# Routing spread over several positions, and output rows added by PE and ACT in place of GpSimd

## The chip, the core and the metric

The kernel runs on one core of one Trainium2 chip. TensorE (PE), VectorE (DVE), ScalarE (ACT), GpSimd (POOL) and SyncE (SP, which only issues DMAs) each run their own list of instructions in order and meet through semaphores. The metric is device time in microseconds; less is better.

## The reference

The input x has 32 sequences of 256 positions and 256 features. What is computed, cut to what matters:

```python
x = x + attn(cond(x, cond_1024))         # causal attention over the 256 positions
y = cond2(x, cond_1024)                  # x + x @ layer, one 256x256 layer per sequence
h1 = y + proj(attention(layernorm(y)))   # over the 32 sequences: 16 heads, 4 of keys
probs = softmax(layernorm(h1) @ router)  # 8 experts, the best 2 are kept
out = x + h1 + moe(layernorm(h1))        # each kept row goes through its experts
```

Here `proj`, `layernorm` and `attention` carry the reference's weights, and `moe` gives each expert at most 2560 rows, in order of the rows.

## The kernel before

It has three stages.

The **opening** (`opening`) runs over the 32 sequences, two at a time (tiles u = 0 and 1), as a software pipeline of steps. A step k makes, for the pair k - 1, the rows x1 on DVE (L1038) from the attention product, the sum `whole` of the base layer and the pair's own (L1044, L1054), and the product of x1 with it, the rows x2. ACT copies x2 from PSUM beside x1 into the tile `x12` (L908), which has columns 0:D for x1 and D: for x2 and eight routing columns. SP stores the two parts into the tensor `x_rows` in DRAM with one DMA each (L568, L580), the x1 part early in the step and the x2 part at its end. At the end of a step DVE takes mean and variance of x2, POOL makes the reciprocal root (L940, L944), and DVE makes `shift` (L1116). Each engine's list has the steps one after the other, so `shift` of a step stands directly before x1 of the next. PE's score product of the new pair (L770 and the three lines of `three` after it) needs the low part of qT (L1027), which DVE makes after the small sums of L1054.

The **rows stage** (the first part of `rows_and_experts`) runs over 64 groups of 128 rows, two at a time, so in 32 positions. SP loads the rows of x_rows into the tile xg (`load`, L1301). At position k PE makes the scores of k (L1469), the projection of k - 2 into the bank `ps_h` (L1484), and turns the weights of k - 1 and multiplies them with the values (L1492, L1505). DVE takes the maxima (L1884), subtracts (L1889), adds projection and xg into `h1` (L1906) and makes the normalizing numbers. ACT makes the exponentials (L1688) and most copies, among them the turned weights (L1703), and writes normalized rows into `kept`. POOL multiplies the weights by their reciprocal sum (L1404), makes the roots, and adds the output rows `res = xg[:, 0:D] + h1` (L1399). SP may store `res` and load the next xg into the same tile only after that addition:

```python
                for u in places:
                    store(j, u)
                    load(j + 1, u)
```

**Routing** works on batches of four positions. When the logits of a batch are there, `choose(m)` on DVE (17 operations on 128x64 or less) finds the two best experts of each row and counts them. PE makes ranks from the counts (L1513), ACT copies them (L1670), and `place(m)` on DVE makes slots and weights (L1831 to L1862). DVE's `step` asks the two generators for one operation after each of its own instructions and runs what is left at the end of the position. From two positions after the choice on, POOL scatters the normalized rows of the batch to their slots, four indirect DMAs per position (L1418).

The **expert stage** runs 39 blocks of rows through two layers in three-part products on PE (L179 to L181), and POOL adds the results to the output in DRAM (L1440).

## Time and profile before

| | |
|---|---|
| three runs | 1207.85, 1207.9 and 1210.3 us, median 1207.9 |
| the profiled execution | 1198.41 us, of which the instructions span 1196.6 us |
| busy in the span | PE 91%, DVE 77%, ACT 66%, POOL 49% |
| mean granted clock of PE | 0.957 |

Busy shares are means over all three stages. A stage's own table of stretches tells which engine is full there. Matmuls are pipelined, so their busy time includes overlaps.

### The profile page before, as it was taken

Reading aid. Unit: us, or ns where it says so; the run is one execution under the profiler, and the core shown is the slowest. Engines: PE = TensorE matmul, PEld = TensorE weight load, DVE = VectorE, ACT = ScalarE, POOL = GpSimd, SP = SyncE. Lnnn points to the kernel's source line nnn. Section 1 sums busy time; section 2 is a strip of 40 time slices with the busy share of each in tenths; the row PEclk is TensorE's granted clock in tenths of the full one; section 3 lists DMA queues with packets and bytes.
Section 4 is the critical chain, followed back from the end, with each engine's and each line's share of the span. In section 5 each row is a group of like instructions: output and inputs, shape, how many; then the busy total and the mean of one; then the engine's idle time right before and its main releaser. Section 6 shows DMA issues by size and latency. Waiting matters only on the chain. (4 is left out here: it accounts for less than half of the span.)

```text
span 1196.6 us, 24516 instructions
## 1 busy us (share of the span) xinstructions
PE 1083.2 (91%) x7906; PEld 993.9 (83%) x7908; DVE 921.7 (77%) x2282; ACT 789.4 (66%) x1776; POOL 585.8 (49%) x568
## 2 busy tenths in 40 slices
PE   7899999999999887788877787899999999999994
PEld 4799999999998677677766765789998889889884
DVE  6677777777775689888998988897777777777772
ACT  2467767677775687677766766566667766776671
POOL 0022212122122154888887786488855554555446
PEclk9999999999999999889788988899999999999997
DMA  8433434334331023444444466478877677777654
GB/s 296 114 115 120 141 111 148 117 128 148 93 96 64 28 81 86 136 130 136 135 136 122 120 179 206 121 208 207 198 185 189 180 185 175 176 182 190 157 141 63
DMA packets 119017, 171.78 MB, mean 144 GB/s; under 512 B 14509, under 2 KB 90189, under 8 KB 118861
## 3 DMA queue, kind: packets, MB, share of 16 engines
q1 hardware_dynamic: 92300, 136.00, 37.1%
q0 software_dynamic: 26592, 34.24, 14.9%
q8 instruction: 64, 1.05, 0.4%
q14 instruction: 61, 0.49, 0.1%
HBM read 104.04 MB, written 67.97 MB: 144 GB/s over the span
## 5 line engine op out<-in xcount | busy, mean ns | idle before, releaser
L1440 POOL DMA_INDIRECT out_rows<-y,row x142 | 233.6, 1645 | 176.5 <-DVE y L2031 136.7
L1962 DVE TENSOR_TENSOR hl<-h,hh 128x512 fp32r<-128x512 f32 (+1 forms) x156 | 99.6, 642 | 84.7 <-ACT h L1641 84.2
L179 PE MATMUL gh<-w2h,hh 128*128 128x256 f32 x568 | 161.0, 284 | 1.1 <-issue 1.1
L181 PE MATMUL gh<-w2h,hl 128*128 128x256 f32 x568 | 161.1, 284 | 0.0
L180 PE MATMUL gh<-w2l,hh 128*128 128x256 f32 x568 | 161.0, 283 | 0.0
L1640 ACT ACTIVATE hh<-gw 128x512 fp32r<-128x512 f32 (+1 forms) x78 | 44.0, 564 | 128.4 <-issue 126.7
L1505 PE MATMUL gw<-pwT,vb 128*128 128x128 f32 x512 | 81.8, 326 | 50.8 <-ACT pwT L1703 48.5
L1418 POOL DMA_INDIRECT slot_rows<-kept,slot x104 | 109.2, 1050 | 29.1 <-issue 27.1
L1505 PEld LDWEIGHTS gw<-pwT,vb 128*128 128x128 f32 x512 | 74.8, 232 | 58.3 <-ACT pwT L1703 55.8
L179 PEld LDWEIGHTS gh<-w2h,hh 128*128 128x128 f32 x568 | 109.1, 192 | 2.3 <-issue 1.2
L180 PEld LDWEIGHTS gh<-w2l,hh 128*128 128x128 f32 x568 | 109.1, 192 | 1.2
L181 PEld LDWEIGHTS gh<-w2h,hl 128*128 128x128 f32 x568 | 109.1, 192 | 0.0
L936 POOL TENSOR_TENSOR layer_low<-whole,layer_high 128x528 fp32r<-128x528 f32 x32 | 41.6, 1320 | 127.2 <-ACT layer_high L856 127.2
L940 POOL TENSOR_SCALAR spread<-mv 128x2 f32<-128x2 f32 x32 | 6.9, 217 | 186.9 <-DVE mv L1110 185.5
L1469 PEld LDWEIGHTS gs<-kvd,qg 64*128 64x128 f32 x512 | 72.2, 202 | 4.4 <-ACT qg L1677 2.1
L1469 PE MATMUL gs<-kvd,qg 64*128 64x128 f32 x512 | 72.0, 284 | 1.2 <-DVE kvd L1874 0.7
L179 PE MATMUL gw<-xh,w1h 128*128 128x512 f32 (+1 forms) x156 | 64.2, 412 | 7.8 <-issue 6.8
L1404 POOL TENSOR_TENSOR pw<-pw,gden 128x512 f32<-128x512 f32 x64 | 65.6, 1042 | 9.5 <-DVE gden L1927 9.5
L1484 PE MATMUL gh<-wproj,aoT 128*128 128x264 f32 x256 | 67.4, 408 | 0.3 <-ACT ranks L1670 0.3
L1472 PE MATMUL gv<-cst,kvd 64*128 64x64 f32 x256 | 65.1, 282 | 0.0
L2031 DVE TENSOR_SCALAR y<-gh,weight 128x256 f32<-128x256 f32 x142 | 59.2, 477 | 5.9 <-PE gh L181 5.6
L1712 ACT COPY aoT<-gw 64x256 f32<-64x256 f32 x128 | 46.6, 364 | 24.7 <-PE gw L1505 22.9
(371 smaller groups left out, 3871.4 us busy)
## 6 DMA issues: line engine op xcount, KB each, us to landing
w1e<-in_moe_w SPq DMA_DIRECT2D x39, 512.0 KB, 5.9
w2e<-in_moe_w SPq DMA_DIRECT2D x39, 512.0 KB, 3.3
xr<-slot_rows SPq DMA_DIRECT2D x32, 532.0 KB, 5.7
xg<-x_rows SPq DMA_DIRECT2D x62, 260.0 KB, 3.4
x_rows<-x SPq DMA_DIRECT2D x32, 264.0 KB, 2.4
xT<-in_xT SPq DMA_DIRECT2D x32, 256.0 KB, 2.7
x<-in_x SPq DMA_DIRECT2D x32, 256.0 KB, 3.6
x_rows<-x SPq DMA_DIRECT2D x32, 256.0 KB, 2.5
```

What stands on the lines that cost most here:

```text
L179: nc.tensor.matmul(out, at_a(ah), at_b(bh), start=first, stop=False, skip_group_check=True)
L180: nc.tensor.matmul(out, at_a(ah), at_b(bl), start=False, stop=False, skip_group_check=True)
L181: return nc.tensor.matmul(out, at_a(al), at_b(bh), start=False, stop=last, skip_group_check=True)
L1404: g.tensor_tensor(pw[k % 2][u][:], pw[k % 2][u][:], den[:, u, :].unsqueeze(2) .broadcast_to([P, TG * NKV, S]), ALU.mult).then_inc(pool_did ...
L1418: g.indirect_dma_start(out=pr.slots, out_offset=bass.IndirectOffsetOnAxis(ap=pr.slot[:, c, j:j + 1], axis=0), in_=pr.rows[:, j, :], in_off ...
L1440: g.indirect_dma_start(out=out, out_offset=bass.IndirectOffsetOnAxis(ap=row[m % NR][:, t:t + 1], axis=0), in_=y[m % 2][:, t, :], in_offset ...
L1469: score = t_.matmul(ps_s[u][:, t * P:(t + 1) * P], qg[u][:, t].rearrange("p j s -> p (j s)"), kvd[u][0:KV1, t].rearrange("p g s -> p (g s) ...
L1472: turned_v = t_.transpose(ps_v[u][:, t * KV1:(t + 1) * KV1], kvd[u][KV1:P, t].rearrange("p g s -> p (g s)"), pr.cst[KV1:P, C_ID + KV1:C_ID ...
L1484: ins = t_.matmul(ps_h[u][:, 0:WIDE], aoT[u][:, h].rearrange("p t s -> p (t s)"), pr.wproj[:, h, :], start=(h == 0), stop=(h == 1))
L1505: ins = t_.matmul(ps_w[u][:, t * P:(t + 1) * P], vb[(k - 1) % 2][u][:, t, :], pwT[u][:, t].rearrange("p j s -> p (j s)"), start=True, stop ...
L1962: v.tensor_tensor(hl[m % 2][:, f, 0:n], h[:, f, 0:n], hh[m % 2][:, f, 0:n].bitcast(F32), ALU.subtract).then_inc(hl_did, 1)
L2031: v.tensor_scalar(y[m % 2][:, t, :], py[half][:, t % 2, :], weight[m % NR][:, t:t + 1], None, ALU.mult).then_inc(y_did, 1)
```

## The change

In the rows stage the output rows come from PE and ACT: the opening stores the sum x1 + x2 in the columns that held x1, PE adds these columns to the projection with a matmul by the identity after DVE has read the bank, and ACT copies the bank to `res`. POOL's addition goes. In the opening DVE makes the sum into the tile `whole` at the end of the step, and the store of it moves there; the next layer sum, which overwrites `whole`, waits for the store.

DVE's routing operations go through a queue that lasts over positions. `choose` joins it after the maxima, `place` at the start of a position, and nothing is run at the end of a position before the last ones. `place` handles both chosen experts in one operation where it took two. POOL's scatters come one position later.

```diff
                 if has(k - 1):
                     for u in places:
-                        after(sp, dve_did["x1"], k - 1, u)
-                        sp.dma_start(dst[seq(k - 1, u)][:, :, 0:D], x12[u][:, :, 0:D]).then_inc(stored1[u], 16)
...
                 if has(k - 1):
                     for u in places:
+                        after(sp, dve_did["sum"], k - 1, u)
+                        sp.dma_start(dst[seq(k - 1, u)][:, :, 0:D], whole[u][:, :, 0:D]).then_inc(stored1[u], 16)
                         after(sp, act_did["x2"], k - 1, u)
                         sp.dma_start(dst[seq(k - 1, u)][:, :, D:], x12[u][:, :, D:]).then_inc(stored2[u], 16)
...
                         dve.wait_ge(x_in[u], 16 * k)
-                        if k > 1:
-                            dve.wait_ge(stored1[u], 16 * (k - 1))
+                        after(dve, dve_did["sum"], k - 2, u)
                         for r in range(TC):
...
                         after(dve, pe_did["layer"], k - 1, u)
                         after(dve, pool_did["layer"], k - 2, u)
+                        if k > 1:
+                            dve.wait_ge(stored1[u], 16 * (k - 1))
                         v.tensor_tensor(whole[u][:, :, 0:D], pc[u][:].rearrange("p (c n) -> p c n", c=DC),
...
                         v.scalar_tensor_tensor(shift[:, u, :], mv[:, u, :, 0], -1.0, rstd[:, u, :],
                                                ALU.mult, ALU.mult).then_inc(dve_did["shift"], 1)
+                        after(dve, act_did["x2"], k - 1, u)
+                        after(dve, pool_did["layer"], k - 1, u)
+                        v.tensor_tensor(whole[u][:, :, 0:D], x12[u][:, :, 0:D], x12[u][:, :, D:2 * D], ALU.add
+                                        ).then_inc(dve_did["sum"], 1)
...
-                    due = first + n + DEPTH + 2 + part
+                    due = first + n + DEPTH + 3 + part
                     if k == (due if due < I2 - 1 else due + 2):
...
-                after(sp, pool_did["res"], j, u)
+                after(sp, act_did["res"], j, u)
                 sp.sem_inc(pr.passed, 1)
...
-                    for u in places:
-                        after(pool, dve_did["h1"], k - 2, u)
-                        if k > 2:
-                            pool.wait_ge(stored[u], 16 * (k - 2))
-                        g.tensor_tensor(res[u][:], rows12(k - 2, u)[:, 0:D], h1[u][:, 0:D], ALU.add
-                                        ).then_inc(pool_did["res"], 1)
...
-                        after(pe, dve_did["h1"], k - 3, u)
+                        after(pe, act_did["res"], k - 3, u)
...
+                if has(k - 2):
+                    for u in places:
+                        after(pe, dve_did["h1"], k - 2, u)
+                        t_.matmul(ps_h[u][:, 0:D], pr.ident, rows12(k - 2, u)[:, 0:D], start=False, stop=True,
+                                  skip_group_check=True).then_inc(pe_did["res"], 1)
                 for m in chosen_at(k - 1):
...
                     pe.wait_ge(chosen_did, m + 1)
-                    after(pe, dve_did["h1"], min(k - 2, I2 - 1), 0)
+                    after(pe, act_did["res"], min(k - 2, I2 - 1), 0)
...
+                if has(k - 2):
+                    for u in places:
+                        after(act, pe_did["res"], k - 2, u)
+                        if k > 2:
+                            act.wait_ge(stored[u], 16 * (k - 2))
+                        a.copy(res[u][:], ps_h[u][:, 0:D]).then_inc(act_did["res"], 1)
                 for m in chosen_at(k - 1):
                     take_ranks(m)
...
-            placing = {}
+            pending = deque()
+
+            def advance():
+
+                while pending and next(pending[0], pending) is pending:
+                    pending.popleft()
...
-                for k in range(K):
-                    rt.step(v.tensor_tensor(eq[:, 0:B], hot[:, k, 0:B], S1[:, 0:B], ALU.mult))
-                    yield
-                    rt.wait()
-                    rt.step(v.tensor_reduce(slotf[:, k, 0:B], eq[:, 0:B], AX.X, ALU.add))
-                    yield
-                    rt.wait()
+                rt.step(v.tensor_tensor(both[:, :, 0:B], hot[:, :, 0:B], S1[:, 0:B].unsqueeze(1).broadcast_to([P, K, B, E]),
+                                        ALU.mult))
+                yield
+                rt.wait()
+                rt.step(v.tensor_reduce(slotf[:, :, 0:B], both[:, :, 0:B], AX.X, ALU.add))
+                yield
+                rt.wait()
...
-                route = chain(*(placing.pop(m) for m in chosen_at(k - 2) if m != LAST_BATCH), *(choose(m) for m in chosen_at(k)))
+                pending.extend(place(m) for m in chosen_at(k - 2) if m != LAST_BATCH)
                 if score:
...
-                        next(route, None)
+                        advance()
+                pending.extend(choose(m) for m in chosen_at(k))
...
-                for _ in route:
-                    pass
-                for m in chosen_at(k - 1):
-                    if m != LAST_BATCH:
-                        placing[m] = place(m)
-                        next(placing[m])
+                while k >= I2 and pending:
+                    advance()
```

The other hunks say the same at more places: three waits of POOL at the end move by one position, `taken` is made by an addition in place of a copy, and the weights of a batch are made in one operation.

## Rows read from the trace of the kernel before

**Rows 1.** Stretches; columns: length, busy PE, PEld, DVE, ACT, POOL, clock, DMA, GB/s.

```profile
74.00:373.00 299.00, 299.00 (x2555) 299.00 (x2554) 220.37 (x561) 210.56 (x505) 63.74 (x88) 1.00 0.38 119
447.60:707.40 259.80, 208.92 (x1466) 182.32 (x1466) 232.67 (x641) 180.06 (x467) 203.95 (x242) 0.88 0.43 128
508.70:516.80 8.10, 7.51 (x64) 6.67 (x63) 8.06 (x29) 6.52 (x17) 6.17 (x8) 1.00 0.47 144
527.60:540.30 12.70, 8.62 (x53) 7.53 (x53) 12.18 (x36) 8.66 (x23) 11.35 (x14) 0.73 0.46 138
```

**Rows 2.** Line L1884, maxima: min/median/max ns, first and last start, two windows.

```profile
L1884 DVE TENSOR_REDUCE gmax<-gs x5: 627/681/692, 405.9 to 421.5; 128x16 f32<-128x512 f32 x5
...
L1884 DVE TENSOR_REDUCE gmax<-gs x52: 658/678/692, 447.6 to 708.7; 128x16 f32<-128x512 f32 x52
```

**Rows 3.** Timeline of DVE, rows stage; columns: start, us, idle before in brackets.

```profile
524.36 0.43 DVE L1906 TENSOR_TENSOR h<-gh,xg 128x264 f32<-128x264 f32 x1 [3.24 <-DMA xg<-x_rows]
...
538.32 1.03 DVE L1814 COPY taken<-chosen 128x64 bf16<-128x64 bf16 x1
```

**Rows 4.** Timeline of POOL, one position of the rows stage.

```profile
526.94 1.40 POOL L1399 TENSOR_TENSOR res<-xg,h 128x256 f32<-128x256 f32 x2
...
530.52 1.08 POOL L1418 DMA_INDIRECT slot_rows<-kept,slot  x1 [0.18 <-issue]
...
535.68 0.26 POOL L1391 TENSOR_SCALAR spread<-mv 128x2 f32<-128x2 f32 x1
...
536.78 1.40 POOL L1399 TENSOR_TENSOR res<-xg,h 128x256 f32<-128x256 f32 x2
```

**Rows 5.** Landings: first of L1301 (loads of xg), then of L568 (stores of x1).

```profile
DMA to landing us min/median/max: 2.7/3.4/5.3
...
DMA to landing us min/median/max: 2.2/2.5/4.5
```

**Rows 6.** Timeline of PE in position 2.

```profile
414.70 2.05 PE L1484 MATMUL gh<-wproj,aoT 128*128 128x264 f32 x8
416.59 1.04 PE L1492 MATMUL gw<-cst,pw 128*128 128x128 f32 x8
418.21 2.05 PE L1505 MATMUL gw<-pwT,vb 128*128 128x128 f32 x16 [0.58 <-ACT pwT L1703]
```

**Rows 7.** Timeline of ACT in position 2.

```profile
415.16 0.63 ACT L1688 ACTIVATE pw<-pw 128x512 f32<-128x512 f32 x1 [1.92 <-DVE pw L1889]
...
417.59 1.05 ACT L1703 COPY pwT<-gw 128x512 f32<-128x512 f32 x2
```

**Rows 8.** Timeline of DVE, start of position 3.

```profile
421.51 0.69 DVE L1884 TENSOR_REDUCE gmax<-gs 128x16 f32<-128x512 f32 x1 [0.36 <-PE gs L1469]
```

**Rows 9.** Timeline of POOL after the last position.

```profile
720.99 0.79 POOL L1391 TENSOR_SCALAR spread<-mv 128x2 f32<-128x2 f32 x1 [4.04 <-DVE mv L1916]
...
728.36 2.47 POOL L1399 TENSOR_TENSOR res<-kvd,h 128x256 f32<-128x256 f32 x2
731.00 1.09 POOL L1418 DMA_INDIRECT slot_rows<-kept,slot  x1 [0.17 <-issue]
```

**Rows 10.** Timeline of DVE, first block of experts.

```profile
740.60 2.49 DVE L1962 TENSOR_TENSOR hl<-h,hh 128x512 fp32r<-128x512 f32 x4
```

**Rows 11.** Timeline of DVE in the opening, from one step to the next.

```profile
266.94 0.16 DVE L1116 SCALAR_TENSOR_TENSOR shift<-mv,rstd 128x2 f32<-128x2 f32 x1 [0.94 <-POOL rstd L944]
267.13 1.66 DVE L1038 SCALAR_TENSOR_TENSOR x<-pa,rden,x 128x256 f32<-128x256 f32 x4
268.70 1.28 DVE L1044 TENSOR_TENSOR whole<-pc,base 128x512 f32<-128x512 f32 x2
270.34 0.40 DVE L1054 TENSOR_TENSOR whole<-pa,base 128x16 f32<-128x16 f32 x2 [0.36 <-PE pa L750]
270.66 1.28 DVE L1027 TENSOR_TENSOR qT_low<-pb,qT_high 128x512 fp32r<-128x512 f32 x2
```

**Rows 12.** Timeline of PE in the opening, first score of the new pair.

```profile
272.11 0.36 PE L770 MATMUL pa<-trir,identr 128*128 128x256 f32 x1
```

More of the change, by code:

```diff
@@ L1 @@
+from collections import deque
 from contextlib import ExitStack
-from itertools import chain
 import numpy as np
@@ L464, in opening @@
         pe_did = {n: sem(f"pe_{n}_") for n in "layer extra qT nT x1T score v kv q pT x2 y".split()}
-        dve_did = {n: sem(f"dve_{n}_") for n in "x1 layer extra qT nT x1T max rden u kv st mv shift v pT".split()}
+        dve_did = {n: sem(f"dve_{n}_") for n in "x1 layer extra qT nT x1T max rden u kv st mv shift sum v pT".split()}
         act_did = {n: sem(f"act_{n}_") for n in "layer qT nT x1T exp v uh q pT x2 nrm".split()}
@@ L564, in step @@
                         sp.dma_start(stack[u][0:STACK], pr.stacks[seq(k, u)]).then_inc(stack_in[u], 16)
-                if has(k - 1):
-                    for u in places:
-                        after(sp, dve_did["x1"], k - 1, u)
-                        sp.dma_start(dst[seq(k - 1, u)][:, :, 0:D], x12[u][:, :, 0:D]).then_inc(stored1[u], 16)
                 if has(k):
@@ L1206, in rows_and_experts @@
         x_in, stored, x_last = sems("g_x_in"), sems("g_stored"), sems("g_x_last")
-        pe_did = {n: sem(f"gpe_{n}_") for n in "score vT wT av h".split()}
+        pe_did = {n: sem(f"gpe_{n}_") for n in "score vT wT av h res".split()}
         dve_did = {n: sem(f"gdve_{n}_") for n in "max sub sum rden h1 st mv shift kv".split()}
-        act_did = {n: sem(f"gact_{n}_") for n in "q exp wT v ao logit nrm".split()}
-        pool_did = {n: sem(f"gpool_{n}_") for n in "soft res spread rstd".split()}
+        act_did = {n: sem(f"gact_{n}_") for n in "q exp wT v ao res logit nrm".split()}
+        pool_did = {n: sem(f"gpool_{n}_") for n in "soft spread rstd".split()}
         L2, eq, S1 = (sb(n, [P, BATCH, E]) for n in ("L2", "eq", "S1"))
@@ L1324, in step @@
                 for u in places:
-                    after(sp, pool_did["res"], j, u)
+                    after(sp, act_did["res"], j, u)
                     if j + 1 < LAST:
@@ L1481, in step @@
                         after(pe, act_did["ao"], k - 2, u)
-                        after(pe, dve_did["h1"], k - 3, u)
+                        after(pe, act_did["res"], k - 3, u)
                         for h in range(2):
                             ins = t_.matmul(ps_h[u][:, 0:WIDE], aoT[u][:, h].rearrange("p t s -> p (t s)"),
-                                            pr.wproj[:, h, :], start=(h == 0), stop=(h == 1))
+                                            pr.wproj[:, h, :], start=(h == 0), stop=(h == 1), skip_group_check=True)
                         ins.then_inc(pe_did["h"], 1)
@@ L1807, in choose @@
                 yield
+                rt.step(v.tensor_tensor(taken[:, :, 1:B + 1].rearrange("p e b -> p b e"), hot[:, 0, 0:B], hot[:, 1, 0:B],
+                                        ALU.add))
+                yield
                 if m == 0:
@@ L1811, in choose @@
                     rt.step(v.tensor_copy(taken[:, :, 0], before[:, :, 2 * BATCHES[m - 1][1]]))
-                yield
-                rt.wait()
-                rt.step(v.tensor_copy(taken[:, :, 1:B + 1].rearrange("p e b -> p b e"), pr.chosen[:, groups, :]))
                 yield
@@ L1855, in place @@
                 rt.wait()
-                for k, out in ((0, eq), (1, L2)):
-                    rt.step(v.tensor_tensor(out[:, 0:B], hot[:, k, 0:B], grow(prob[:, k, 0:B]), ALU.mult))
-                    yield
+                rt.step(v.tensor_tensor(both[:, :, 0:B], hot[:, :, 0:B], prob[:, :, 0:B].unsqueeze(3).broadcast_to([P, K, B, E]),
+                                        ALU.mult))
+                yield
                 rt.wait()
-                v.tensor_copy(pr.rows[:, groups, D:D + 2].bitcast(I32), pr.tok[:, groups, :])
+                rt.step(v.tensor_copy(pr.rows[:, groups, D:D + 2].bitcast(I32), pr.tok[:, groups, :]))
                 yield
-                v.tensor_tensor(pr.rows[:, groups, D + 2:ROW], eq[:, 0:B], L2[:, 0:B], ALU.add).then_inc(routed, 1)
+                rt.wait()
+                v.tensor_tensor(pr.rows[:, groups, D + 2:ROW], both[:, 0, 0:B], both[:, 1, 0:B], ALU.add).then_inc(routed, 1)
                 yield
@@ L1891, in step @@
                                         ALU.subtract).then_inc(dve_did["sub"], 1)
-                        next(route, None)
+                        advance()
+                pending.extend(choose(m) for m in chosen_at(k))
                 if has(k + 1):
@@ L1895, in step @@
                         heads(k + 1, u)
-                        next(route, None)
+                        advance()
                 if norm:
                     for u in places:
-                        after(dve, pool_did["res"], k - 3, u)
                         after(dve, act_did["nrm"], k - 3, u)
@@ L1907, in step @@
                                         ).then_inc(dve_did["h1"], 1)
-                        next(route, None)
+                        advance()
                     for u in places:
@@ L1911, in step @@
                         v.bn_stats(stats[:, u, :], h1[u][:, 0:D]).then_inc(dve_did["st"], 1)
-                        next(route, None)
+                        advance()
                     after(dve, pool_did["spread"], k - 3, U2 - 1)
@@ L1924, in step @@
                         v.tensor_reduce(den[:, u, :], pw[k % 2][u][:], AX.X, ALU.add).then_inc(dve_did["sum"], 1)
-                        next(route, None)
+                        advance()
                         after(dve, dve_did["sum"], k, u)
                         v.reciprocal(den[:, u, :], den[:, u, :]).then_inc(dve_did["rden"], 1)
-                        next(route, None)
+                        advance()
                 if norm:
```

12 lines of the change are left out of this document (6 added, 6 removed).

## The prediction

> **What bounds the kernel now.** I read the table of stretches first, because the shares of the whole span are a mean over three stages. In the opening the PE is busy for all 299.00 of 299.00 us at a granted clock of 1.00 [rows 1]: there a microsecond is lost for good if it is put between two matmuls, and nothing taken from another engine is won. In the middle stage, which makes the rows, no engine is full: in 447.6 to 707.4 PE has 208.92 of 259.80 us, DVE 232.67, POOL 203.95, and the clock is 0.88 [rows 1]. The first score maximum of each position marks its start. Positions 1 and 2, which route and scatter nothing, take (421.5 - 405.9) / 2 = 7.8 us; from position 6 to the start of position 31, where the last maximum but one stands 1.3 us before the 708.7 of the row, 25 positions take 259.8 us, 10.39 each [rows 2]. The expert stage after it is untouched in its order.
>
> Three things fill the gap between 7.8 and 10.39, one after the other in a cycle of four positions. First, where a batch is chosen (527.6 to 540.3) the position takes 12.7 us, DVE is busy for 12.18 of them, PE for 8.62, and the clock falls to 0.73 [rows 1]: all 17 routing operations go into this one position, the last of them behind DVE's other work, with PE waiting. One of these, a small copy, takes 1.03 us [rows 3]. Two positions after a choice (508.7 to 516.8) the 12 operations that place a batch are interleaved with DVE's other work, and the position takes 8.1 us [rows 1], so interleaving is cheap. Second, POOL runs without a pause: 536.78 - 526.94 = 9.84 us from one addition of output rows to the next, of which the four scatters take 535.68 - 530.52 = 5.2 and the two additions 1.40 [rows 4]. Third, DVE waits 3.24 us for the xg rows [rows 3]: their load may be issued only after POOL's addition has read the tile, and it lands 3.4 us later as a median, 5.3 at most [rows 5].
>
> **The change part by part: the middle stage.** *Additions off POOL.* 2 x 0.70 = 1.40 us per position leave POOL [rows 4]; its cycle with scatters becomes 9.84 - 1.40 = 8.44.
>
> *Additions onto PE.* Two fp32 matmuls of 256 columns per position. The nearest row is the projection: four matmuls of 264 columns (eight records) start at 414.70, and the next line starts at 416.59, so 0.47 us each [rows 6]; two make 0.94, 0.91 for 256 columns. They stand between the last product of a position and the first score of the next. In position 2 that place is on the ring that sets the time: score, maximum, subtraction, ACT's exponential at 415.16, its copies until the transposed weights at 417.59, PE's product at 418.21 for 2 us, the next score, the next maximum at 421.51, which DVE waits for [rows 6 to 8]. Nothing in the ring has slack, so all 0.91 us count: 7.8 + 0.91 = 8.7 us. They are not hidden.
>
> *Additions onto ACT.* Two PSUM copies of 128x256; a pair of 128x512 takes 1.05 us [rows 7], so between half of that and all of it; I take 0.76. ACT waits 1.92 us for DVE before its first exponential in position 2 [rows 7], and this hides them; without that cover they would add 0.76 to the ring. The load of xg now goes out after these copies and no longer after 9.84 us of POOL; it has more than half of a ring of 8.7 us to land in 3.4, so the wait of 3.24 us goes. In the rare case of 5.3 us some of it comes back.
>
> *Routing spread.* Choosing (17 operations) and placing (now 10) go into 14 gaps of a position, over two positions. By the placing position, 12 gaps lengthen DVE to 8.1 us [rows 1], which lies inside 8.7: nothing. Two extras stay. A choosing operation that meets POOL's multiplication may grow as the copy at 1.03 us did [rows 3]; I give the choosing position 0.6. In the position after, PE's rank product waits for ACT's copy of row tile 0; I give it 0.5, between nothing and a copy plus its queue of 0.76. So a cycle of four is about 8.7 + 8.8 + 9.2 + 9.3, mean 9.0. From below the ring alone gives 8.7; from above, DVE with everything exposed gives about 9.4.
>
> Sum: 25 x (10.39 - 9.0) = 35 us won. Positions 1 to 5 take 447.6 - 405.9 = 41.7 us now [rows 2] and will take 5 x 8.75 = 43.8, 2 lost. Net 33 won, with 23 to 40 as ends.
>
> *Scatters one position later.* In the body POOL scatters in the same gaps. At the end four scatters more, 5.2 us, come after the last position. They fall partly where the additions of the last rows were (2.47 us from 728.36), before the first scatter at 731.00 [rows 9]: of eight scatters from 728.4 on, 1.3 us apart, the last goes out at 737.5. DVE's rest of the hidden layer, which waits for that batch, begins at 740.60 [rows 10]; 3.1 us are left for a landing, beside medians of 2.5 and 3.4 [rows 5]. I take 0; 5 if the cover is gone.
>
> **The change part by part: the opening.** Each of 16 steps gains two DVE additions of 128x512, 0.64 us each by the row of the pair of layer sums at 1.28 [rows 11]. The first lies in the 0.94 us in which DVE waits for POOL's second root [rows 11] and is free. The second pushes the x1 rows from 267.13 to 267.77. DVE had 0.36 us of waiting before the next small sums, so the low part of qT that PE needs is ready at about 271.6 in place of 271.3, and PE asks for it at 272.11 [rows 11, 12]. So far nothing is lost.
>
> But the store moved too. It now sends `whole` at the end of the step, and the layer sum, which overwrites `whole`, waits for it to land. Queued behind that sum on DVE are the other layer sum, the small sums and the low part of qT, and PE's score waits for the last. The second tile's store can be issued at 267.77. Landing x us later, the chain is 267.77 + x + 0.64 + 0.32 + 0.64, which must not pass 272.11: x up to 2.7 us is free. SP's queue also orders it behind two other stores of that size issued within about 1 us. The stores of these columns land today after 2.2 us at least, 2.5 as a median, 4.5 at most [rows 5]; I take 3.7, nearer to the upper end, for a transfer behind others. Then POOL: DVE's first new addition runs beside POOL's spread and root. A spread that met DVE work on two SBUF tiles took 0.79 us [rows 9] and one that didn't 0.26 [rows 4], so up to 0.53 may come on top; I take 0.3. Cost per step 3.7 + 0.3 - 2.7 = 1.3 us; 14 steps with a full PE and a wait make 18 us. Ends: 0 (2.2 and no lock), and 14 x (4.5 + 0.53 - 2.7) = 33.
>
> The Trainium skill, page "SBUF — State Buffer", section "Who interferes with whom", has DVE and GpSimd share one port pair as an exclusive lock, and its section on the two sides of SBUF counts a DVE operation with two SBUF inputs among the holders. The new addition is one; the row of 0.79 us agrees, and by the rule the blocked side waits the whole addition, up to 0.64 in place of my 0.3, 23 us in place of 18, which stays in the first case below.
>
> **Rivals.** *The opening is free.* The stores land in 2.2 to 2.7 us even third in the queue. For it: the median of 2.5 [rows 5]. Against: half of the landings are later than these, and the queue is now three deep. Time: 1207.9 - 33 = 1175.
> The Trainium skill, page "DMA: Bandwidth & Descriptors", section "Anatomy of one DMA", fits a transfer that GpSimd issues as 2.0 us plus its bytes by 436e3; for 256 KB this is an estimate of 2.6 us, which is the free case; the maximum of 4.5 us in the row shows that the stores of SP don't keep to it here.
>
> *The store wait eats everything (the other side).* From 33 / 14 = 2.4 us per step on the kernel is slower. For it: landings of 4.5 exist [rows 5], and one behind two such may be later still. Against: the shorter ones are as many. At 2.8 us: 39 lost, 1207.9 - 33 + 39 = 1214.
>
> *POOL holds the middle stage.* Its 8.44 us are 97% of 8.7; a late spread makes a late shift, ACT's normalizing and so the next exponential late. At 9.8 us a position 15 - 2 = 13 are won: 1207.9 - 13 + 18 = 1213. Against: POOL no longer adds anything when it is behind.
>
> *The end holds the experts.* 5 us of scatters show: 1207.9 - 33 + 18 + 5 = 1198.
>
> **How the numbers follow.** The profiled execution took 1198.41 us with a span of 1196.6; the three runs have a median of 1207.9, so 0.8% above. The sum, -33 + 18 = -15, gives a span of about 1182 and, against the median, 1193 us. Chances: this case 0.53, opening free 0.20, store wait 0.10, POOL 0.12, the end 0.05. Those of no gain are at 1213 and 1214; leaving out a tenth on either side, the range is 1176 to 1213. About 0.2% (2.4 us) can be told from no change. Faster: 0.53 + 0.20 + 0.04, less 0.02 of the first case; same 0.09, from the edges of three cases; slower 0.16.
>
> **What would show it.** Right: positions of 8.7 to 9.3 us, with none of 12.7, and the clock near 1.0 in the middle stage; no wait of DVE for xg; idle PE before scores in the opening, with steps over 22 us, and DVE waiting at the layer sum for the store. Wrong: steps still at 21.3, then 1175; or positions at 9.8 with PE waiting for POOL's multiplication or ACT for the shift; or an opening longer by over 33 us.

## The result and the profile after

The changed kernel takes 1190.3 us as a median of four runs (1181.2 to 1193.8), the kernel before 1207.9 in the same session: a ratio of 0.987, 95% interval 0.982 to 0.992. The forecast was 1193. The profiled execution of the changed kernel took 1190.1 us with a span of 1188.3, 8.3 us shorter than that of the kernel before, and both come from one execution each.

First the stretches of the changed kernel, to be held against [rows 1]: the opening, the 25 positions from position 6 on, and then the four positions of one cycle (place, plain, choosing, after the choice). Columns: length, busy PE, PEld, DVE, ACT, POOL, clock, DMA, GB/s.

```profile
74.00:382.00 308.00, 304.17 (x2561) 300.27 (x2559) 234.24 (x592) 212.42 (x506) 68.82 (x88) 1.00 0.37 115
460.80:695.60 234.80, 207.50 (x1569) 178.07 (x1568) 214.52 (x616) 194.35 (x512) 162.49 (x185) 0.99 0.47 137
517.10:525.70 8.60, 8.01 (x63) 6.93 (x62) 8.53 (x27) 6.73 (x17) 5.50 (x7) 1.00 0.49 143
525.70:534.40 8.70, 8.11 (x65) 7.01 (x63) 7.78 (x18) 7.78 (x21) 7.19 (x10) 1.00 0.52 155
534.40:543.40 9.00, 8.41 (x68) 7.28 (x68) 8.85 (x27) 7.61 (x20) 7.12 (x8) 1.00 0.54 156
543.40:553.80 10.40, 8.11 (x64) 6.84 (x64) 8.77 (x27) 9.06 (x26) 8.97 (x10) 1.00 0.44 137
```

The 25 positions took 259.8 us before [rows 1] and take 234.8. The choosing position no longer stands out: DVE is busy for 8.85 us in it, not 12.18, and the clock is 1.00, not 0.73. The long position of a cycle is now the one after it. In the opening PE is no longer full: 304.17 of 308.00 us.

From both traces, the way of the 8.3 us: the second x1 of the opening comes 0.9 later (among all profiled executions it comes between 76.3 and 85.9), the opening from there to the first maximum of the rows stage, where position 0 begins, grows from 324.1 to 333.0 us (+8.9), the rows stage up to its last position shrinks from 307.0 to 285.4 (-21.6), from there to the first block of experts it is 9.7 in place of 8.3 (+1.4), the blocks take 439.4 in place of 442.2 (-2.8), and the end behind the last block's first copy 43.6 in place of 38.7 (+4.9). The sum is -8.3. The last term cannot be put down to the change, as the last section shows.

DVE in the opening, from one step to the next, to be held against [rows 11] (start, us, operation; in brackets the idle time before and what ended it), and SP's issues of the same time:

```profile
272.20 0.16 DVE L1115 SCALAR_TENSOR_TENSOR shift<-mv,rstd 128x2 f32<-128x2 f32 x1
272.28 0.71 DVE L1119 TENSOR_TENSOR whole<-x 128x512 f32<-128x512 f32 x1
273.60 0.16 DVE L1115 SCALAR_TENSOR_TENSOR shift<-mv,rstd 128x2 f32<-128x2 f32 x1 [0.61 <-ACT nrm L912]
273.68 0.69 DVE L1119 TENSOR_TENSOR whole<-x 128x512 f32<-128x512 f32 x1
274.28 1.65 DVE L1035 SCALAR_TENSOR_TENSOR x<-pa,rden,x 128x256 f32<-128x256 f32 x4
275.89 0.69 DVE L1043 TENSOR_TENSOR whole<-pc,base 128x512 f32<-128x512 f32 x1
277.48 0.69 DVE L1043 TENSOR_TENSOR whole<-pc,base 128x512 f32<-128x512 f32 x1 [0.90 <-DMA x_rows<-whole]
```

```profile
273.02 0.40 SPq L576 DMA_DIRECT2D x_rows<-whole  x1
273.46 1.09 SPq L578 DMA_DIRECT2D x_rows<-x  x1
...
274.59 0.47 SPq L576 DMA_DIRECT2D x_rows<-whole  x1
```

The predicted wait is there: the second layer sum (L1043) waits 0.90 us for the store of the second sum to land. Over the opening DVE waits 12.5 us in this way, 17 times. SP issued that store behind the x2 store of the first tile. The low part of qT comes behind that sum, and PE starts the score of the next pair [rows 12] as soon as its first tile is ready, as predicted:

```profile
278.25 1.28 DVE L1025 TENSOR_TENSOR qT_low<-pb,qT_high 128x512 fp32r<-128x512 f32 x2
278.98 0.38 PE L768 MATMUL pa<-trir,identr 128*128 128x256 f32 x1
```

In four steps PE also waits at an earlier place, which the prediction did not name: its transposes of x1 (L709) need the same layer sum (us in all, times, longest).

```profile
PE pc L709 <- DVE whole L1043: 2.9, 4, 1.0
```

The second `shift` is put down to ACT, but it starts 0.04 us after POOL's root ends:

```profile
272.56 1.00 POOL L942 TENSOR_TENSOR rstd<-spread,half 128x2 f32<-128x2 f32 x1
```

This root runs beside the first new addition and takes 1.00 us; the one before it, without the addition, takes 0.71.

ACT and PE in the position after a choice, 543.4 to 553.8:

```profile
545.68 0.21 ACT L1665 ACTIVATE ratio<-ratio 128x8 f32<-128x8 f32 x1 [0.66 <-DVE ratio L1815]
545.80 0.61 ACT L1691 ACTIVATE pw<-pw 128x512 f32<-128x512 f32 x1
```

```profile
552.21 0.19 PE L1516 MATMUL gh<-chosen,strictb 128*128 128x64 bf16 x1 [0.45 <-ACT res L1722]
```

The first large exponential (L1691) stands behind a small one (L1665, the chances of the chosen batch), which waits for an operation of the choice that DVE now makes in this position. And PE's rank product waits 0.45 us for ACT's copy of the output rows.

### The profile page after: what moved, and what is told of

Read it like the earlier page. It is cut to its first block and busy times, and to the rows that moved or that the text cites. A ratio compares the mean times of both kernels' runs of the same rounds, so it can differ in the third digit from the quotient of the medians.

```text
span 1188.3 us, 24750 instructions
## 1 busy us (share of the span) xinstructions
PE 1094.4 (92%) x8034; PEld 996.9 (84%) x8036; DVE 920.2 (77%) x2290; ACT 811.3 (68%) x1840; POOL 549.9 (46%) x504
## 5 line engine op out<-in xcount | busy, mean ns | idle before, releaser
L1438 POOL DMA_INDIRECT out_rows<-y,row x142 | 237.7, 1674 | 173.3 <-DVE y L2042 79.9
L1503 PE MATMUL gw<-pwT,vb 128*128 128x128 f32 x512 | 69.2, 291 | 30.9 <-ACT pwT L1706 28.6
L1503 PEld LDWEIGHTS gw<-pwT,vb 128*128 128x128 f32 x512 | 62.8, 200 | 38.5 <-ACT pwT L1706 35.9
L1467 PEld LDWEIGHTS gs<-kvd,qg 64*128 64x128 f32 x512 | 67.6, 190 | 4.0 <-ACT qg L1680 2.1
L1467 PE MATMUL gs<-kvd,qg 64*128 64x128 f32 x512 | 68.2, 274 | 1.2 <-DVE kvd L1889 0.7
L1623 ACT ACTIVATE xh<-gs,ln 128x512 fp32r<-128x512 f32 (+1 forms) x78 | 58.8, 758 | 5.6 <-PE gs L187 5.6
L1629 ACT ACTIVATE xTe<-gs,ln 128x512 f32<-128x512 f32 (+1 forms) x78 | 62.4, 804 | 0.0
```

Of the source, the lines that this page charges most:

```text
L1438: g.indirect_dma_start(out=out, out_offset=bass.IndirectOffsetOnAxis(ap=row[m % NR][:, t:t + 1], axis=0), in_=y[m % 2][:, t, :], in_offset ...
L1467: score = t_.matmul(ps_s[u][:, t * P:(t + 1) * P], qg[u][:, t].rearrange("p j s -> p (j s)"), kvd[u][0:KV1, t].rearrange("p g s -> p (g s) ...
L1503: ins = t_.matmul(ps_w[u][:, t * P:(t + 1) * P], vb[(k - 1) % 2][u][:, t, :], pwT[u][:, t].rearrange("p j s -> p (j s)"), start=True, stop ...
L1629: ins = a.activation(xT[:, c, 0:n], pt[c][:, 0:n], ACT.Identity, scale=pr.ln2[:, 0, c:c + 1], bias=pr.ln2[:, 1, c:c + 1])
```

## The experiments

Each is the changed kernel with the edit shown, if nothing else is said. Ratios are to the kernel before, run on the same chip, whose medians were 1201.8 to 1206.3 us there. Single runs of one kernel differ by up to some 20 us, so where an effect is under 1% the verdict is read from the steps and positions of the profile. "Opening" is from the second x1 to the first maximum of the rows stage (324.1 before, 333.0 changed), "stage" from there to the last position (307.0 and 285.4), "25 positions" those from position 6 (259.9 and 234.8). Six of these 25 stand after a choice (the expectations count a seventh, behind them).

**The sums stored first.**

```
 for u in places:
     ... store sum of u
+for u in places:
     ... store x2 rows of u
```

> The changed kernel, with SyncE's two stores of the sums issued before the two stores of the x2 rows (in place of sum 0, x2 0, sum 1, x2 1). Theory A, the opening loses 8.9 us because the second layer sum waits for the second tile's store, and that store is late because it stands behind the x2 rows: the steps that now take 21.9 to 23.1 us fall to 21.6 or less, the wait of the layer sum for the store (12.5 us in all) falls by half or more, and the opening wins about 4 us. Theory B, the loss is the additions themselves (DVE's 0.7 us each, and POOL's root that grew from 0.71 to 1.00 us beside them): steps as before, 21.9 as a mean, no change. In the whole time both lie within 0.4%.

Theory A. All but one of the steps from the third on are 21.31 or 21.32 us, as in the kernel before; the opening is 326.3 us, 6.8 of the 8.9 us are back. The size varies: the profiled executions of six other runs below that have the opening of the changed kernel took 329.4 to 333.3 us there, and the three with the sums first 326.3 each, so the order is worth 3 to 7 us, and the change costs the opening 5 to 9. The layer sum now waits 0.19 us where it waited 0.90:

```profile
278.17 1.65 DVE L1036 SCALAR_TENSOR_TENSOR x<-pa,rden,x 128x256 f32<-128x256 f32 x4
279.76 0.69 DVE L1044 TENSOR_TENSOR whole<-pc,base 128x512 f32<-128x512 f32 x1
280.64 0.69 DVE L1044 TENSOR_TENSOR whole<-pc,base 128x512 f32<-128x512 f32 x1 [0.19 <-DMA x_rows<-whole]
```

It starts 2.47 us after x1, 3.20 in the changed kernel. The landings of the sums' stores, in this run and then in the changed kernel:

```profile
DMA to landing us min/median/max: 2.1/2.2/3.1
```

```profile
DMA to landing us min/median/max: 2.2/2.5/4.2
```

In these steps the additions on DVE, POOL's slower root and a sum that starts 2.47 us after x1 cost nothing; the other 2.2 us lie in the second step, the one step of 22.02 and the end of the opening. The run: 1187.2 us, ratio 0.984 (0.977 to 0.990).

**The sum in another tile.**

```
-v.tensor_tensor(whole[u][:, :, 0:D], x12[u][:, :, 0:D], x12[u][:, :, D:2 * D], ALU.add)
+v.tensor_tensor(x[u][:], x12[u][:, :, 0:D], x12[u][:, :, D:2 * D], ALU.add)
 ... the load of the next x moves behind the stores and waits for the sum's store
```

> The changed kernel, with DVE's sum of x1 and x2 written into the tile that held the input rows x, and no longer into the tile of the layer sums; the next load of x waits for the store in place of the layer sum. All work is still done. Theory A (the store's landing is what the opening pays): the steps go back to 21.3 to 21.5 us, the last x1 rows of the opening come about 8 us earlier (375 in place of 382.6), the kernel wins 7 to 9 us (0.6 to 0.75%). Theory B (the additions on DVE are what it pays): steps stay at 21.9 as a mean, no gain. Third, the loads of x, issued some 5 us later, come too late for the x1 rows: DVE waits there for x; the slack is over 10 us, so this is not expected.

None of the three as sized: 1291.5 us, ratio 1.073 (1.067 to 1.078), steps of 27.6 to 30.0 us. The slack of 10 us was a misreading: the next x1 follows the sum at once on DVE, so a load issued behind the store has no time at all, and x1 waits for it:

```profile
311.04 0.88 DVE L1036 SCALAR_TENSOR_TENSOR x<-pa,rden,x 128x256 f32<-128x256 f32 x2 [4.44 <-DMA x<-in_x]
```

It decides nothing between A and B, but shows what a wait in this place costs: 4.44 and 0.96 us of waiting in a step, and steps some 7 us longer.

**The opening of the kernel before.**

```
+sp.dma_start(dst[seq(k - 1, u)][:, :, 0:D], x12[u][:, :, 0:D])   # early in the step
-sp.dma_start(dst[seq(k - 1, u)][:, :, 0:D], whole[u][:, :, 0:D])
-v.tensor_tensor(whole[u][:, :, 0:D], x12[u][:, :, 0:D], x12[u][:, :, D:2 * D], ALU.add)
 ... x1 waits for the store, the layer sum for none
```

> The changed kernel with the opening of the kernel before: the x1 rows are stored as soon as they are made, DVE makes no sum, and the layer sum waits for no store. The output rows then lack the x2 term, while every operation of the rows stage stays. This is the whole cost of the change in the opening: by either theory the steps are 21.32 us, the last x1 rows come at 373.7 and the kernel wins 9 us against the changed one (0.75%). If it wins no more than 3 us, what is lost in the opening is given back later, and if it wins over 14 the sums cost something outside the opening too.

The opening is 324.1 us, to a tenth that of before, and the 25 positions take 234.6: what the change costs in the opening is 8.9 us and is not given back later. 1182.4 us, ratio 0.981 (0.975 to 0.988).

**The chances behind the exponentials.**

```
-for m in chosen_at(k - 1): chances(m)      # ahead of exponentials(0)
 exponentials(0)
 ...
 exponentials(1)
+for m in chosen_at(k - 1): chances(m)
```

> The changed kernel, with ACT's exponential of the ratio (the chances of a chosen batch) moved from the head of ACT's position to behind both large exponentials. Theory C: the position after a choice takes 10.33 us and not the predicted 9.3 because this small operation waits for DVE's ratio, which now is made in that position, and the first large exponential is queued behind it (1.0 us late). Then the seven positions of 10.33 us fall to 9.3, and the kernel wins 7 us (0.6%). Theory D: these positions are long because PE's rank product waits for ACT's copy and because DVE has more work; then they stay at 10 us or more and the gain is under 2 us.

Theory C, with 0.78 in place of 1.0 us: each of the six positions after a choice takes 9.54 to 9.56 us (10.33), the 25 positions 229.4, the stage 280.1. 1179.4 us, ratio 0.979 (0.974 to 0.985).

**The rank product ahead of the additions.**

```
+after(pe, dve_did["h1"], ...); rank product of the batch
 for u in places: ps_h[u] += ident x xg[u]
-after(pe, act_did["res"], ...); rank product of the batch
```

> The changed kernel, with PE's rank product of a chosen batch put in front of the two additions of the output rows, so that it waits for DVE's hidden rows (as before the change) and no longer for ACT's copy of the first row tile. Theory C, what is left of the long position after a choice: with the chances where the changed kernel has them the position is 10.33 us; the wait of 0.45 us of the rank product goes, and the position falls to 9.9, seven times, 3 us in all (0.25%), not to be told in the whole time from the spread of the runs, but from the positions. Theory D, nothing waits for the rank product in that position and the next score is held by the chances alone: 10.33 stays.

The rank product now stands between the projection and the addition in one bank, and the output rows of this run come out changed; every operation is still made, and only the times are read. Three of the positions after a choice take 9.72 us and one 9.82, a gain of 0.6 (0.45 expected); the two others take 11.35 and 11.36, with a granted clock of 0.85 in them:

```profile
508.50:518.20 9.70, 7.69 (x59) 6.59 (x59) 8.68 (x26) 8.61 (x24) 8.47 (x9) 1.00 0.44 126
544.80:556.10 11.30, 9.30 (x59) 7.84 (x58) 8.64 (x25) 8.72 (x24) 9.58 (x11) 0.85 0.39 119
```

So C holds where the clock does. 1184.4 us, ratio 0.987 (0.983 to 0.992).

**Each half alone.** The routing half is the kernel before with the new `choose`, `place`, `advance` and the scatters one position later; the addition half is the changed kernel with the old `choose`, `place` and the flush at the end of the position (its scatters stay one position later).

> The kernel before with the first half of the change alone: the routing operations spread over the gaps of following positions and the scatters one position later, while GpSimd still makes the output rows and the opening is that of before. Theory E: the choosing position falls from 12.7 us to GpSimd's 9.84, the positions beside it stay at 9.4 to 9.9, none gets down to 8.7; the 25 positions from 6 on take 235 + 11 = 246 us or a little less (259.9 before), the kernel wins about 14 us and is near 1193. Theory F, each half is nothing without the other: GpSimd makes up in the next position what DVE wins, the 25 positions stay over 255 us.

> The changed kernel with the routing order of the kernel before: all operations of a choice in its one position, flushed at its end, the placing operations two positions later, while PE and ACT make the output rows and the sums are made in the opening. Theory E: the choosing position stays at 12 us or more because DVE is full in it, the wait for the xg rows goes, plain positions are at 8.7; a cycle of four is about 12.2 + 9.9 + 8.7 + 8.7 = 39.5 us against 40.5 before, so the 25 positions take 245 to 252 us, and with the 9 us that the opening pays the kernel is at 1202 to 1210, no clear gain. Theory F: without GpSimd's additions the choosing position shrinks by itself to 10 or 11 us, and the kernel is under 1198.

Routing alone: 1200.6 us, ratio 0.997 (0.993 to 1.001). Its 25 positions take 249.3 us, and many of them 9.86 to 9.89, which is POOL's round from one addition to the next:

```profile
523.82 1.40 POOL L1400 TENSOR_TENSOR res<-xg,h 128x256 f32<-128x256 f32 x2
...
533.68 1.40 POOL L1400 TENSOR_TENSOR res<-xg,h 128x256 f32<-128x256 f32 x2
...
543.56 1.40 POOL L1400 TENSOR_TENSOR res<-xg,h 128x256 f32<-128x256 f32 x2
```

The choosing position takes 9.86 to 10.85 us, the one after it 10.2 to 11.9 at clocks of 0.71 to 0.84. This is theory E, with 10.6 us won in the 25 positions in place of 14. But in the whole time it cannot be told from no gain (the interval holds 1): over the whole stage it is 7.5 us, and 4.2 of them go again between the last position and the last block, because POOL's scatters, one position later and behind its last additions, hold DVE's rest of the hidden layer:

```profile
745.49 2.50 DVE L1967 TENSOR_TENSOR hl<-h,hh 128x512 fp32r<-128x512 f32 x4 [5.70 <-DMA slot_rows<-kept,slot]
```

The interval between blocks there is 22.1 us, 18.2 in the kernel before and in the changed one. Additions alone: 1207.2 us, ratio 1.006 (1.002 to 1.010). DVE is busy for 10.48 of the 11.00 us of a choosing position (12 were expected by E, 10 or 11 by F), the position after it takes 9.4 to 11.0, the 25 positions 249.2, and the opening pays its share:

```profile
549.40:560.40 11.00, 9.57 (x75) 8.24 (x75) 10.48 (x35) 9.08 (x24) 8.46 (x11) 1.00 0.51 144
560.40:569.80 9.40, 6.56 (x51) 5.53 (x50) 8.05 (x19) 7.64 (x23) 7.29 (x9) 1.00 0.41 128
```

In the 25 positions the halves win 10.6 and 10.7 us alone and 25.1 together, so E sized each half about right, and F is left with 3.8 us: each half removes one of two bounds, POOL's 9.86 us in every position or DVE's 11.00 in one of four. Over the whole stage it is 7.5 and 4.1 against 21.6, but the rest of that gap lies in positions 1 to 5. They take 41.6 us before, 45.0 in the changed kernel, 44.7 with the routing half and 48.2 with the addition half; positions 1 and 2 had clocks of 0.82 and 0.68 in the one half, 0.67 and 0.71 in the other, and position 1 varies by up to 2.8 us among the runs, whatever the edit.

**Both mends.** The stores' order and the place of the chances, as above.

> The changed kernel with both mends: the two sums stored before the x2 rows, and the chances behind the large exponentials. If the two gains add (6.5 us in the opening from steps of 21.32 us, 5.4 us in the positions after a choice at 9.55), it is 12 us faster than the changed one, about 1178, a ratio to the kernel before of 0.977; if the stores' order helped by chance of that run only, steps of 21.9 come back and it is like the run with the chances alone.

In the profile they add: steps of 21.32 us (one of 21.99), opening 326.3, the 25 positions 226.4, stage 275.5. In the whole time the sum is not shown: 1176.7 us, ratio 0.981 (0.976 to 0.987), where 0.977 was expected and the chances alone gave 0.979.

**And ACT's first output copy earlier.**

```
 values(0)
+if chosen_at(k - 1): output(0)
 values(1)
-output(0)
 output(1)
```

> The kernel with both mends (sums stored first, chances behind the exponentials), and in the positions after a choice ACT copies the first tile of output rows before, not behind, the second tile of attention values, so that PE's rank product waits less for that copy. Theory C: the wait of 0.45 us goes or falls to 0.1, and the position after a choice falls from 9.55 us to 9.1; seven times, 3 us, 1174 where the kernel with both mends is at 1177 (0.25%, to be read from the positions). Theory D: the second tile of attention values now is late and holds the projection of the next position, or the shift holds ACT's normalizing; 9.5 stays.

The rank product waits for nothing any more and the position after a choice takes 9.22 to 9.24 us (9.55), in each cycle; the 25 positions 224.2, stage 274.7. That is theory C with 0.33 of the 0.45 us. In the whole time it can't be seen: 1181.3 us, ratio 0.981 (0.977 to 0.986).

**What PE's additions cost.** They are left out, ACT copying the projection alone; then with the xg rows loaded when DVE has the hidden rows; then with the chances moved as well.

```
-t_.matmul(ps_h[u][:, 0:D], pr.ident, rows12(k - 2, u)[:, 0:D], start=False, ...)
 ... second run, SP:
-after(sp, act_did["res"], j, u); load(j + 1, u); store(j, u)
+after(sp, dve_did["h1"], j, u); load(j + 1, u)     # both tiles, then both stores
```

> The changed kernel without PE's two additions of the output rows: ACT copies the projection alone, so the output rows lack x1 and x2. This measures what the two matmuls of 256 columns cost. Theory G, the prediction's (the ring of score, exponential, attention values and next score sets the time, nothing in it is hidden): plain positions fall from 8.67 us to 7.8 everywhere, the 25 positions from 6 on win about 20 us. Theory H, GpSimd's work of a position with four scatters (8.25 to 8.7 us from scatter to scatter in the changed kernel) is a second bound just below: 7.8 us in the positions without scatters (2 to 5), 8.3 to 8.7 in those with them, so that the additions cost little there and the 25 positions win under 8 us.

> The changed kernel without PE's two additions (the output rows lack x1 and x2), and with the next xg rows loaded as soon as DVE has made the hidden rows, no longer behind ACT's copies of the output rows; both loads of a position now stand before both stores. Without the additions alone, two positions took 7.8 us and the next 10.0, where DVE waited 1.90 us for the xg rows and the granted clock was 0.82 in the position after. Theory I, the late rows and the clock after the stall ate the 20 us: now the waits for xg go, positions 2 to 5 are at 7.8 us, the later plain ones at 8.3 to 8.7 under GpSimd's scatters, the 25 positions from 6 on take 215 to 222 us (239.6 without the early load, 234.8 with the additions). Theory J, PE that has less to do is granted less clock by itself: the clock of the stage stays at 0.94 and the 25 positions over 232 us, though no xg rows are waited for.

> The run without PE's additions and with the early loads (the output rows lack x1 and x2), and now with the chances behind the large exponentials as well. Theory I, continued: in that run the position after a choice took 11.5 us because PE waited 2.53 us in one piece behind ACT's late exponential and its clock was 0.85 in that position (its product 3.29 us in place of 2.05); with the wait 0.8 us shorter the clock stays at 1.00, these positions fall to 9.0 or less, the plain ones stay at 8.0 to 8.6, and the 25 positions from 6 on take 215 to 222 us (226.4 with the additions and the same mend). Theory J, the clock falls wherever PE has less to do: the positions after a choice stay over 10.3 us and the 25 positions over 226 us.

Without the additions the kernel is no faster than with them: 1198.0 us, ratio 0.991 (0.987 to 0.996). Theory G's 20 us are not there. Position 2 does take 7.8 us (position 1 has no additions in either kernel); in position 3 DVE waits for xg rows, and in position 4 the clock is 0.82 (the profiled execution took 1205.8 us, so only these first positions are read from it):

```profile
446.71 0.43 DVE L1918 TENSOR_TENSOR h<-gh,xg 128x264 f32<-128x264 f32 x1 [1.90 <-DMA xg<-x_rows]
```

```profile
432.40:440.20 7.80, 7.21 (x61) 6.37 (x60) 7.62 (x18) 6.08 (x16) 2.03 (x4) 1.00 0.00 1
440.20:450.20 10.00, 9.27 (x75) 8.17 (x74) 7.69 (x18) 7.80 (x21) 2.80 (x4) 1.00 0.38 100
450.20:459.60 9.40, 6.71 (x44) 6.14 (x43) 7.59 (x18) 7.42 (x20) 4.00 (x6) 0.82 0.21 65
```

With the early loads (1188.7 us, 0.989) plain positions take 7.95 us without scatters and 8.2 to 8.6 with them, much as theories H and I said (that GpSimd's work bounds them was not tried), but five of the six after a choice take 11.5 to 12.3 and the 25 positions 238.4. In one of those PE waits 2.53 us in one piece, and its clock is 0.85 in the position; in the changed kernel PE waits 1.83 us at the same place and the clock stays at 1.00 (the last section shows that the length of this wait does not decide it). First the run without additions, then the changed kernel:

```profile
550.27 3.29 PE L1507 MATMUL gw<-pwT,vb 128*128 128x128 f32 x16 [2.53 <-ACT pwT L1706]
```

```profile
548.84 2.05 PE L1503 MATMUL gw<-pwT,vb 128*128 128x128 f32 x16 [1.83 <-ACT pwT L1706]
```

With the chances moved too (1176.7 us, 0.974, 0.969 to 0.979) four of these six take 9.5 us at a clock of 1.00, and the two undisturbed cycles (positions 16 to 23) take 35.5 and 35.2 us, against 36.1 and 35.9 for the same positions of the kernel with both mends and the additions. Theory I holds for the direction there, not for its figures of 9.0 and 215 to 222. In the two others the clock still fell, to 0.78 and 0.73, with 11.0 and 12.3 us, and the 25 positions take 228.1, between the 226.4 and 229.4 of the two runs that have this mend and the additions: against the former, five positions at clocks of 0.73 to 0.81 lose 5.6 us and the other twenty win 3.8. Theory J has that much for it.

## Why the prediction was right, and where its terms were off

The sign, the mechanism of both halves and the number were right. The number was partly luck: two terms were too large with opposite signs, and the medians lie 17.6 us apart where the two profiled executions, from which the terms are read, lie 8.3 apart.

**Middle stage, 33 us won, measured 21.6.** The plain position came out as worked out: 8.7 predicted, 8.67 to 8.90 measured in all but two, and so did the placing (8.8 against 8.68 or 8.69 in all but one) and the choosing position (9.2 against 8.9 to 9.3).

The wait of the hidden rows for xg [rows 3] was to go and did so only in part. In the 25 positions it was 8.8 us in 5 waits before, and the list of waits of the changed kernel puts 5.1 us in 7 waits down to nothing (`issue`). But in the six longest of these the hidden rows begin 0.08 us after the second tile's load of xg has landed. First the two lists (us in all, times, longest), then the longest wait and its load, which took 6.0 us to land, in one of the two long positions near the end:

```profile
DVE h L1906 <- DMA xg<-x_rows: 8.8, 5, 3.2
```

```profile
DVE h L1921 <- issue: 5.1, 7, 1.5
```

```profile
666.31 0.34 SPq L1305 DMA_DIRECT2D xg<-x_rows  x1
672.38 0.43 DVE L1921 TENSOR_TENSOR h<-gh,xg 128x264 f32<-128x264 f32 x1 [1.54 <-issue]
```

The prediction named such a case, with a landing of 5.3 us; but a load that lands in its 3.4 us has a wait of 0.73 us behind it too, so "more than half of a ring" was not left for it. That position takes 8.81 us, so most of the wait is hidden.

The term that was mis-sized is the position after a choice, 9.3 predicted and 10.33 measured. The prediction gave it 0.5 for the rank product, which waits 0.45 us; it missed that the operations moved into this position have a reader on ACT that stands at the head of ACT's list. Moving that reader took 0.78 us off, moving ACT's copy 0.33 more. The six such positions, five of 10.3 and one of 11.39 at a clock of 0.85, are 7 us of the 10 that the 25 positions (234.8) lie over 25 x 9.0; two more positions near the end, of 10.24 (the one with the late load) and 10.35, the latter at a clock of 0.84, make 3. Positions 1 to 5 take 45.0 us in place of the forecast 43.8.

**All 0.91 us of PE's additions count.** True for the first position that has them (7.81 without, 8.67 with). Not true for a cycle: without the additions, and with what then was late next taken away, an undisturbed cycle is 0.6 or 0.7 us shorter, not 3.6, and in the profiled execution more than that went again in positions at a lower clock. The step "nothing has slack" was read from a position without scatters and choices [rows 6 to 8].

**POOL.** It does not hold the stage: that rival is refuted for the changed kernel, and the run with the routing half shows what it would have been, 9.87 us a position.

**End of the rows stage, 0.** DVE's rest of the hidden layer waits 2.31 us for the scatters, and the interval between blocks is 18.2 us, as before: hidden. The routing half alone shows the cost when POOL's additions still stand ahead of the scatters, 22.1, so the cover that the prediction named was the right one.

**Opening, 18 us lost, measured 8.9** (5 to 9 in the profiled executions of all runs with that opening). The mechanism is shown by the order of two issues: the store's landing behind the x2 store. The term that was mis-sized is x, the time from x1 to the layer sum that waits. It was taken as 3.7 us in every step; it is 2.5 to 4.4, 3.1 on average, so a step costs 0.5 us on average in place of 1.3, and the steps are 21.2 to 23.1 us, not all over 22. That up to 2.7 us are free nearly holds: 2.54 goes with a step of 21.32, 2.72 with 21.42, 3.20 with 21.90, 4.42 with 23.10. The lock between DVE and POOL was sized right, 1.00 - 0.71 = 0.29 us, and costs nothing, since the steps of 21.32 in the run with the sums first have it too. By the Trainium skill, page "SBUF — State Buffer", section "Who interferes with whom", the port pair that DVE and GpSimd share is an exclusive lock, for which a DVE instruction with two SBUF inputs and a GpSimd instruction that reads SBUF contend. The trace agrees: the root began at 272.56 and the addition ended at 272.99, so 0.43 us of it were left to wait for, not the whole, and the root lost 0.29. The estimate of 2.6 us for a transfer that GpSimd issues, from the Trainium skill, page "DMA: Bandwidth & Descriptors", section "Anatomy of one DMA", lies within what the stores take when they go first (2.1 to 3.1, median 2.2); in the changed kernel the longest took 4.2.

What is left open: why position 1 takes 7.8 us in some runs and 9.1 to 10.5 in others; its clock was 1.00 in the former and 0.63 to 0.82 in the latter, 0.67 in the changed kernel. And why that load of xg took 6.0 us, and the position behind it 10.35 us, was not tried.

## What to carry to other kernels

When operations move to a later place in one engine's list, look up every reader of their results, and where in its own list each reader stands: a 0.2 us operation at the head of ACT's list cost 0.78 us in every cycle here. Try each half of a change alone, and read it in the same stretch of the profile: in the 25 positions the halves won 10.6 and 10.7 us and together 25.1, while in the whole time neither half alone was faster (0.997 and 1.006). Where a later store must land before a buffer is written again, issue it ahead of the stores that nobody waits for.

## What the runs showed of the hardware

**Less work on PE, lower clock.** Over positions 6 to 29 the granted clock was 1.00 with the chances mended, and 0.95 with the same mend and no additions on PE, in stretches of nearly the same length:

```profile
459.10:679.50 220.40, 195.72 (x1502) 168.25 (x1501) 206.02 (x589) 186.28 (x494) 157.06 (x178) 1.00 0.47 137
```

```profile
455.10:674.20 219.10, 186.08 (x1412) 162.57 (x1411) 205.43 (x588) 186.01 (x493) 155.87 (x176) 0.95 0.44 136
```

PE has 9.6 us less to do by its busy time, and the stretch is 1.3 us shorter. The mean clock of whole executions goes the same way: 0.978 to 0.988 in the six of the kernel with the chances mended and 0.968 to 0.977 in the four with that mend and no additions, 0.973 to 0.982 in the four of the changed kernel and 0.962 to 0.973 in the ten without its additions. Why is not shown. The length of PE's wait in a position does not settle it: waits of 2.53 and 1.83 us went with 0.85 and 1.00 above, but one of 1.91 us in the changed kernel with 0.85 (position 23) and one of 2.45 us in the run with the chances mended with 1.00 (the same position):

```profile
622.62 2.90 PE L1503 MATMUL gw<-pwT,vb 128*128 128x128 f32 x16 [1.91 <-ACT pwT L1706]
```

```profile
618.03 2.05 PE L1503 MATMUL gw<-pwT,vb 128*128 128x128 f32 x16 [2.45 <-ACT pwT L1705]
```

**An end with two lengths.** From the last block's first copy to the end the profiled executions took either 38.5 to 38.9 us (the kernel before and six of the variants) or 43.5 to 44.2 (the changed kernel and six variants). In the long ones POOL waits for its own additions to land in block after block (61.9 us in all in the changed kernel, 21.7 in that with both mends) and stays a landing behind; in the last block DVE then waits for it:

```profile
1162.43 0.88 DVE L2042 TENSOR_SCALAR y<-gh,weight 128x256 f32<-128x256 f32 x2 [1.93 <-PE gh L181]
1167.80 1.66 DVE L2042 TENSOR_SCALAR y<-gh,weight 128x256 f32<-128x256 f32 x4 [4.49 <-POOLq L1446]
```

So 4.9 us of the difference between the two profiled executions come from this. They cannot be put down to the change, since variants that differ from the changed kernel in an earlier stage alone ended either way. What decides between the two is not known.
